# Box sums of the max/average chain by accumulating transfers inside SBUF, and low parts on VectorE, in a fused pooling, convolution and attention kernel

## The reference, cut to what matters

```python
# x: (8, 256, 32, 32)
x_aux = silu(conv1x1(gn(x), w_sta) + b_sta)         # 128 channels
y1 = [x_aux]; y2 = [x_aux]
for _ in range(3):
    y1.append(0.9 * maxpool5x5(y1[-1]) + 0.1 * sumpool5x5(y1[-1]) / 25)    # the max/average chain
    y2.append(rwpool(y2[-1]))                        # exp-weighted pooling, 5x5
y = concat([silu(conv1x1(concat(y1), w_cv1)), silu(conv1x1(concat(y2), w_cv2))])   # 512 channels
a = depthwise 1x3, 3x1, dilated 1x3, dilated 3x1 of y
a = conv1x1(a, w_c1)
x = x + silu(conv1x1(y * a, w_cvend))
f = tokens(gn(x)); q = f @ w1.T
x = x + from_tokens(softmax(q @ f.T / 16) @ (f @ w2.T))
```

## Time and profile before

| | us |
|---|---|
| median of 3 runs | 1584.52 (1584.18 to 1590.7) |
| the profiled execution, its own time | 1581.99 |
| its span | 1580.2 |
| mean granted TensorE clock | 0.909 of full |

### The profile page before, as it was taken

The page is one execution under the profiler, slowest core; times in us unless marked ns, Lnnn a source line. Parts: engine busy times, 40 slices in busy tenths (PEclk is TensorE's granted clock), DMA queues, the critical chain, the costliest instruction groups (busy, mean ns, idle before and its releaser), DMA issues.

```text
span 1580.2 us, 19005 instructions
## 1 busy us (share of the span) xinstructions
PE 1315.6 (83%) x7156; PEld 1095.1 (69%) x7156; DVE 1188.2 (75%) x1167; ACT 715.2 (45%) x773; POOL 336.5 (21%) x138
## 2 busy tenths in 40 slices
PE   3647485677399998999889989998998999999797
PEld 1247475674276887688669858975887688778687
DVE  7659496777868987897699769886988697796443
ACT  0346363455235542653375335534642653465233
POOL 0657585750101020102010210201020102012000
PEclk9768687778599999999999999999999999999999
DMA  7323232221000011001000200020011001000100
GB/s 281 128 94 120 80 108 104 69 118 54 0 27 14 1 52 43 14 1 67 28 14 13 82 9 7 14 81 14 1 40 55 14 1 67 27 1 1 54 1 27
DMA packets 22656, 76.10 MB, mean 48 GB/s; under 512 B 1968, under 2 KB 4656, under 8 KB 22576
## 3 DMA queue, kind: packets, MB, share of 16 engines
q1 hardware_dynamic: 21872, 74.59, 13.0%
q10 hardware_dynamic: 704, 0.30, 0.1%
HBM read 49.71 MB, written 25.17 MB: 47 GB/s over the span
## 4 chain that ended last, share of the span: by engine, by line
issue 55%; PE 11%; POOL 6%; DVE 5%; ACT 1%; POOLq 0%; DVEq 0%; ACTq 0%
POOL q_all L1050 4%; PE slot L1170 3%; PE slot L1132 3%; PE ps_o L1170 2%; POOL f_all L1059 2%; DVE a L1445 2%; DVE between L1445 2%; PE slot L1186 1%; PE slot L1110 0%; POOL c_rstd L1055 0%; PE slot L533 0%; DVE c_minus_max L1454 0%; PE ps_ot L1202 0%; ACT a L1302 0%; ACT pooled L1311 0%
## 5 line engine op out<-in xcount | busy, mean ns | idle before, releaser
L1170 PE MATMUL slot<-f_all,q_all 128*128 128x512 f32 x768 | 193.5, 403 | 13.4 <-ACT pooled L1311 13.4
L1170 PE MATMUL ps_o<-v_all,pt_all 128*128 128x256 f32 x1536 | 200.2, 287 | 5.4 <-ACT mixed L1330 5.2
L1050 POOL TENSOR_TENSOR q_all<-a,f_all 128x1024 fp32r<-128x1024 f32 x32 | 81.4, 2580 | 537.1 <-ACT f_all L1321 537.1
L1445 DVE SCALAR_TENSOR_TENSOR a<-between,k_columns,a 128x992 f32<-128x992 f32 (+1 forms) x128 | 191.5, 1502 | 4.9 <-ACT a L1302 2.6
L1170 PEld LDWEIGHTS ps_o<-v_all,pt_all 128*128 128x128 f32 x1536 | 189.8, 192 | 7.6 <-DVE pt_all L1449 6.2
L1170 PEld LDWEIGHTS slot<-f_all,q_all 128*128 128x128 f32 x768 | 142.7, 192 | 43.1 <-ACT pooled L1311 14.8
L1325 ACT CAST v_all<-y 128x1024 fp32r<-128x1024 f32 x32 | 33.6, 1051 | 191.3 <-DVE y L1467 191.3
L1110 PE MATMUL slot<-wide,k_cv 128*128 128x512 f32 x256 | 114.3, 597 | 0.0
L1449 DVE TENSOR_TENSOR pt_all<-slot,pt_all 128x1024 fp32r<-128x1024 f32 x64 | 78.1, 1221 | 47.6 <-ACT pt_all L1316 47.6
L533 PE MATMUL ps_e<-box,e_hi 128*128 128x192 f32 (+2 forms) x240 | 45.0, 349 | 72.6 <-DVE newton L766 45.2
L1055 POOL TENSOR_TENSOR c_rstd<-c_spread,k_minus_half 128x2 f32<-128x2 f32 x8 | 5.6, 696 | 463.6 <-DVE gmean L1506 463.6
(11 more groups left out here) (163 smaller groups left out, 3019.1 us busy)
## 6 DMA issues: line engine op xcount, KB each, us to landing
y_in<-levels SPq DMA_DIRECT2D x24, 512.0 KB, 3.6
levels<-y_out SPq DMA_DIRECT2D x24, 512.0 KB, 2.7
x_all<-in_x SPq DMA_DIRECT2D x8, 1024.0 KB, 13.2
q_all<-levels SPq DMA_DIRECT2D x8, 1024.0 KB, 4.9
x<-in_x SPq DMA_DIRECT2D x8, 1024.0 KB, 4.9
out<-x SPq DMA_DIRECT2D x8, 1024.0 KB, 5.3
wide<-levels SPq DMA_DIRECT2D x8, 512.0 KB, 3.3
pooled<-levels SPq DMA_DIRECT2D x8, 512.0 KB, 3.3
```

Source lines behind the costliest of these rows:

```text
L1050: nc.gpsimd.tensor_tensor(a_lo[:, k], a[:, k], a_hi[:, k].bitcast(F32), ALU.subtract).then_inc(a_lo_done.sem, 1)
L1170: last = nc.tensor.matmul(out, lhs, rhs, start=(n == 0), stop=(n == len(parts) - 1))
L1445: nc.vector.scalar_tensor_tensor(o, u, keep["taps"][:, s, c, tap:tap + 1], o, ALU.mult, ALU.add).then_inc(taps.sem, 1)
```

## The change

For `phase_c`, the box sum of a level is no longer computed on TensorE. ScalarE copies the level into `row_sums` (`begin_rows`), and GpSimd issues four transfers from SBUF to SBUF that add the level, shifted by +1, -1, +2 and -2 words, to that copy (`add_rows`), each after the one before has landed. ScalarE copies the result to `box_sums` (`begin_columns`), and four more transfers add the row sums, shifted by the same numbers of rows (`add_columns`). That is 24 transfers and 6 copies an image. So that a shift by a word doesn't run into the neighbouring row, the levels have two zero words after each row of 32 (`PITCH` 34, `PADDED` 1092 words). `phase_a` computes each stem a second time in this layout and stores it to a second HBM tensor, `padded`; level 0 of the next image is loaded from it into its own tile, `chain.first`, after the present image's whole chain is done, and into `chain.wide` later, as before. The low parts `f_lo` and `a_lo` move from GpSimd to VectorE. All order in the queues around the chain is rewritten: the maxima of level 0 stand first in VectorE's pass, those of level 1 among the attention tiles, the third mixture last. The diff, cut to its core:

```diff
+PITCH = W + 2
+ROWS = H * PITCH
+PADDED = 2 + ROWS + 2
+SHIFTS = (1, -1, 2, -2)
+    def begin_rows(self, act, i, level):
+        if level:
+            wait(act, self.done, i, MIX * level)
+        else:
+            wait(act, self.first_in, i, 16)
+            wait(act, self.done, i - 1, MIX * LEVELS)
+        self.nc.scalar.copy(self.row_sums[:, 0:ROWS], self.source(level)[:, 2:2 + ROWS]).then_inc(self.rows_begun.sem, 1)
+    def begin_columns(self, act, i, level):
+        wait(act, self.rows_added, i, 4 * 16 * (level + 1))
+        self.nc.scalar.copy(self.box_sums[:, 0:ROWS], self.row_sums[:, 0:ROWS]).then_inc(self.columns_begun.sem, 1)
+    def add_rows(self, pool, i, level):
+        for n, d in enumerate(SHIFTS):
+            if n:
+                wait(pool, self.rows_added, i, 16 * (4 * level + n))
+            else:
+                wait(pool, self.rows_begun, i, level + 1)
+            pool.sem_inc(self.gate, 1)
+            pool.dma_start(self.row_sums[:, 0:ROWS], self.source(level)[:, 2 + d:2 + d + ROWS],
+                           accum_op=ALU.add).then_inc(self.rows_added.sem, 16)
...
# phase_a, ScalarE: silu(n, u)
+                nc.scalar.activation(chain.rows_of(stem_rows[u]), image2d(ps[:, u]), ACT.Silu, bias=keep["b_sta"]).then_inc(rows_done, 1)
                 nc.scalar.activation(stem[u][:, :], ps[:, u], ACT.Silu, bias=keep["b_sta"]).then_inc(stem_done, 1)
...
# phase_c, SyncE
                 if chained:
+                    wait(sp, chain.done, i, MIX * LEVELS)
+                    sp.sem_inc(chain.gate, 1)
+                    if attn:
+                        wait(sp, chain.rows_added, i, 4 * 16 * LEVELS)
+                        sp.sem_inc(chain.gate, 1)
+                    sp.dma_start(chain.first[:, :], padded[i + 1]).then_inc(chain.first_in.sem, 16)
                     wait(sp, cv, i, 2 * CT)
                     load_chain(i + 1)
...
# phase_c, GpSimd
             def step(i, conv, attn, chained):
+                if chained:
+                    chain.add_rows(pool, i + 1, 0)
                 if attn:
                     wait(pool, norm, i - 1, 4)
                     nc.gpsimd.tensor_tensor(rstd[:, :], spread[:, :], keep["minus_half"][:, 0:CT], ALU.pow).then_inc(rstd_done.sem, 1)
-                if attn and conv:
-                    for t in range(CT):
-                        wait(pool, f_hi_done, i - 1, t + 1)
-                        nc.gpsimd.tensor_tensor(f_lo[:, t], a[:, t], f_hi[:, t].bitcast(F32), ALU.subtract).then_inc(f_lo_done.sem, 1)
-                if conv:
-                    for n in range(KT):
-                        inputs_lo(i, n)
+                if chained:
+                    chain.add_columns(pool, i + 1, 0)
+                    for level in range(1, LEVELS):
+                        chain.add_rows(pool, i + 1, level)
+                        chain.add_columns(pool, i + 1, level)
...
# phase_c, ScalarE
+                if chained:
+                    chain.begin_rows(act, i + 1, 0)
...
+                        if chained and k == 1:
+                            chain.begin_columns(act, i + 1, 0)
...
-                        if chained and t == TURN_AT + 1:
-                            level_hi(0)
+                        if chained and t == 2:
+                            chain.begin_rows(act, i + 1, 1)
+                        if chained and t == 6:
+                            chain.begin_columns(act, i + 1, 1)
...
                     gated_hi(0)
                     if chained and attn:
-                        level_hi(1)
-                    gated_hi(1)
+                        chain.begin_rows(act, i + 1, 2)
+                    for m in range(1, KT):
+                        gated_hi(m)
...
+                if chained:
+                    if not attn:
+                        chain.begin_rows(act, i + 1, 2)
+                    chain.begin_columns(act, i + 1, 2)
...
# phase_c, VectorE
+                if chained and attn:
+                    level_maxima(0)
                 if attn:
                     small = Steps(dve, norm, i - 1)
                     wait(dve, group_mean, i - 1, 1)
...
-                        if chained and t == TURN_AT + 1:
-                            level_lo(0)
-                        if chained and 0 < t < TILES - 1:
-                            level_maxima(0, *([0, 1] if t == 1 else [t]))
+                        if chained and t == 2:
+                            level_mixture(0)
+                            level_maxima(1, 0, 1)
+                        if chained and 2 < t < TILES - 1:
+                            level_maxima(1, t - 1)
...
                     turned_lo(TILES - 1)
+                    if conv:
+                        for n in range(KT):
+                            inputs_lo(n)
...
                 if chained and attn:
-                    level_lo(1)
+                    level_maxima(1, 6)
+                    level_mixture(1)
...
                     for m in range(CT):
                         nc.vector.bn_aggr(mv[:, m, :], stats[:, m].rearrange("p h s -> p (h s)")).then_inc(bn.sem, 1)
+                if chained:
+                    level_mixture(2)
```

More of the change, by code:

```diff
@@ L185, in maxima @@
     def maxima(self, dve, i, level, *steps):
-        src, pairs, tall = self.inner(level), self.pairs, self.tall
+        alone = isinstance(i, int) and i == 0
+        first = False if alone else level == 0
+        src, pairs, tall = self.rows_of(self.first) if first else self.inner(level), self.pairs, self.tall
         m4, four = image2d(self.work_b[:, :]), image2d(self.work_a[:, 0:N])
@@ L229, in mixture_of_sums, with mixture_of_boxes @@
         self.mixture(dve, 0, level, self.sum_b[:, :, :])
-    def mixture_of_boxes(self, dve, i, level, slot):
-        wait(dve, self.boxed, i, level + 1)
-        self.mixture(dve, i + 1, level, image2d(slot))
+    def mixture_of_boxes(self, dve, i, level):
+        wait(dve, self.columns_added, i, 4 * 16 * (level + 1))
+        boxes = self.box_sums[:, 0:ROWS].rearrange("p (h w) -> p h w", w=PITCH)[:, :, 0:W]
+        self.mixture(dve, i, level, boxes)
 class Pooled:
@@ L283, in split_lo, with phase_a @@
                                      ALU.subtract).then_inc(self.lo_done.sem, 1)
-def phase_a(nc, x, w, consts, keep, levels, rmc, box, chain, pooled):
+def phase_a(nc, x, w, consts, keep, levels, padded, rmc, box, chain, pooled):
     with ExitStack() as ctx:
@@ L300, in phase_a @@
         stem = (pooled.second, chain.work_b)
+        stem_rows = (chain.row_sums, chain.box_sums)
         raw, at = {}, 0
@@ L331, in phase_a @@
         max_done = sem("a_max_done")
+        rows_set, rows_done = sem("a_rows_set"), sem("a_rows_done")
+        rows_stored = [sem(f"a_rows_stored{u}") for u in range(2)]
         box_ready = sem("a_box_ready")
@@ L365, in _ @@
                     store(pair * 2 + u, u)
+            for u in range(2):
+                sp.wait_ge(rows_stored[u], 16 * (B // 2))
         @block.scalar
@@ L430, in _ @@
             nc.gpsimd.memset(keep["minus_half"][:, :], -0.5).then_inc(rstd_done, 1)
+            for u in range(2):
+                nc.gpsimd.memset(stem_rows[u][:, :], 0.0).then_inc(rows_set, 1)
             chain.set_sum_borders()
@@ L861, with phase_c @@
 BEFORE = KT * STAGES - TILES
-TURN_AT, BOX_AT = 1, TILES - 2
 ORDER = (2, 3, 0, 1)
-def phase_c(nc, x, out, keep, levels, box, chain, pooled):
+def phase_c(nc, x, out, keep, levels, padded, chain, pooled):
     with ExitStack() as ctx:
@@ L1087, in claim @@
                     return slots_of[kind, k]
-                def turn_level(level):
-                    wait(pe, *((chain.done, i + 1, MIX * level) if level else (chain.loaded, i + 1, 16)))
-                    slot = claim("zt", level)
-                    for m in range(N // P):
-                        last = nc.tensor.transpose(slot[:, cols(m)], chain.wide[:, level, cols(m)], keep["ident"][:, :])
-                    last.then_inc(chain.turned.sem, 1)
-                def box_level(level):
-                    wait(pe, chain.hi_done, i, level + 1)
-                    slot = claim("zb", level)
-                    box_sum(nc, pe, box, slot, zt_hi, zt_lo,
-                            (chain.lo_done.sem, chain.lo_done.at(i, level + 1))).then_inc(chain.boxed.sem, 1)
                 def cv1(m, between=None):
@@ L1108, in cv1 @@
                                 wait(pe, chain.done, i, MIX * k)
-                            rows = chain.wide[:, k, h * HALF:(h + 1) * HALF]
-                            last = nc.tensor.matmul(slot[:, h * HALF:(h + 1) * HALF], keep["cv1"][:, k, cols(m)], rows,
+                            rows = chain.inner(k)[:, h * (H // 2):(h + 1) * (H // 2)]
+                            last = nc.tensor.matmul(image2d(slot[:, h * HALF:(h + 1) * HALF]), keep["cv1"][:, k, cols(m)], rows,
                                                     start=(k == 0), stop=(k == KT - 1))
@@ L1612, in _, with program @@
```

(4 more changed lines are left out.)

169 lines of the change are left out of this document (73 added, 96 removed).

## The result

The changed kernel takes 1716.8 us (median of 4 runs, 1714.2 to 1722.7) against 1587.2 (4 runs) for the kernel before: 1.082 times as long, 95% interval 1.078 to 1.086. The profiled execution took 1717.15 us with a span of 1715.3.

A forecast was written before the change was run, and what follows sets the result against it. TensorE was taken to bound the image loop (136.6 of 147.6 us). Span 429.3 + 16D + 6(123.2 + 7D) + 197.4 + 6 = 1371.9 + 58D, 1673.5 at D = 5.2, so 1678 us; 8 in 10: 1605 to 1845.

The forecast's parts named there:

- the loop: Rival 1: 24 serial transfers per image bind, pass 34.4 + 23D above D = 5.55, span 839.1 + 154D; chance 0.3.
- D: Time of one accumulating transfer on GpSimd's queue, semaphore to semaphore: taken as 5.2 us, bounds 3.0 and 6.5.
- M: End of VectorE's third mixture in a pass, forecast at s + 116.8 + 4D.
- The formula of a pass, 123.2 + 7D: One image-loop pass: 116.8 + 4D from s to M plus 6.4 + 3D to next s; 159.6 us at D = 5.2.
- s: End of VectorE's c_shift, where a pass's attention starts; forecast M + 6.4 + 3D, 22.0 us behind M.
- ce: TensorE's second output product in a pass; its end was forecast 113.1 us after s, down from 118.8.
- Rival 4: TensorE's clock drops after two new idle stretches per pass, up to 2.3 us each, adding 28: 1706; chance 0.08.
- 512.5 + 6 for stage one: First pass: M of image 1 at 429.3 + 16D, 512.5; plus 6 (bounds 0 and 12) for computing stems twice.
- 6.1 us behind M [...] instead of 20.1: Pass 7, which has no chain: its s comes 6.1 us behind M instead of 20.1, making the tail 197.4.
- The break-even: Transfer time at which change costs nothing: D = 3.5 against a 147.6 us pass, 3.6 for the whole kernel.
- 5.8 us on the way to ce: Gain from s to end of "ce": 3.9 for TensorE's box sums off the path, the rest from low parts.
- 6.3 of 9.3 (3.9 + 2.4): TensorE's box-sum work per pass, 9.3 us: 3.9 on the path ahead of "ce", last box sum's 2.4 behind it.

The follow-up runs named there:

- hybrid_rstd: Changed kernel with level 2 back on TensorE, c_rstd between second and third row transfer of level 0, ScalarE's level-0 box_sums copy one product earlier: 1551.2 us.
- rstd_early: Changed kernel with c_rstd moved on GpSimd's queue from behind the fourth row-transfer issue of level 0 to between the second and third: 1671.5 us.
- plain: Changed kernel with its transfers as plain copies, the adding left out (box sums wrong in content): 1607.4 us.
- no_boxes: Kernel before with low parts on VectorE and the third stage's box sums left out altogether: 1444.0 us, 0.910 of before.
- hybrid_128: hybrid_rstd with 96 unused bytes behind box_sums, so large tensors start at multiples of 128 bytes: 1537.2 us, 0.973 of before.
- after_128: Changed kernel with 96 unused bytes behind box_sums, so large tensors start at multiples of 128 bytes: 1719.0 us.
- after: The changed kernel itself, against the kernel before: 1716.8 us, 1.082 times as long.
- aligned: Changed kernel with 32 unused bytes behind box_sums, so tensors from pairs on start at multiples of 64 bytes: 1711.6 us, 1.081 of before.

## Why the prediction was right, and where it was off

The forecast was 1678 us, and 1716.8 lies in its range and on its side. It forecast 91 us more than before, and 130 were measured. That the result lies in the range is in part luck: the range reached to 1845 for the case of a dearer transfer, with the loop binding. D came out as forecast and the loop didn't bind; the 39 us came from terms beside D. By the formula it would have taken a D of 5.9.

Of the signs, these held: transfers 5 us apart, c_shift 23.4 us behind M (22 forecast), and no wait of VectorE for column sums in the attention tiles. TensorE was busy for 135.3 us of a pass and not 127, with three idle stretches at the border and not two.

**D.** 5.2 taken, 5.17 measured. The reason given, that the destination is read too, fits the plain copies: they halve the DMA engines' share, and land in 3.0 us instead of 4.7, as the slope of the rows had it (1.7 for 544 KB more). The number came out by two errors that cancel. The 5.1 worked out from the 1 MB rows was the time from issue to landing, which measured 4.5 to 4.7, and the 0.5 us from a landing to the next issue was not added to it. The Trainium skill (pages "DMA: Bandwidth & Descriptors", "Anatomy of one DMA", and "Collectives: The Full Stack", "The bandwidth ceiling: the fold count and why AG ≠ RS ≠ AR") gave an estimate of 4.6 for a transfer; the landing, 4.5 to 4.7, agrees with it.

**The formula of a pass, 123.2 + 7D.** Its shape held: two steps changed by experiment gave 8.2 us (for 6.8 expected) and 20.8 (for 4D = 20.7, though by other parts, as told above). Its constant was 5.7 us too small, 165.3 for 159.6, which is 34 of the 42 us by which span and forecast (1715.3, 1673.5) differ. Over the three parts of the pass that ends at M = 1008.40: s to the end of ce took 114.4 for 113.1, ce to M 26.0 for 24.5, and M to s 23.3 for 22.0. From ce to M one cause shows in rows, and I had left it out: the row transfers of level 2 are on the path, since mixture 3 waits for them and not only for "ce". The first of them meets a 1 MB load that SyncE issues at the same time (SyncE's queue, the chain that ended last, ScalarE):

```profile
956.07 0.41 SPq L1086 DMA_DIRECT2D out<-x  x1
960.27 0.38 SPq L1089 DMA_DIRECT2D x<-in_x  x1
...
960.00 9.07 DMA row_sums<-wide
969.63 5.18 DMA row_sums<-wide
975.37 4.86 DMA row_sums<-wide
...
985.51 1.10 ACT L180 COPY box_sums<-row_sums 128x1088 f32<-128x1088 f32 x1 [1.78 <-DMA row_sums<-wide]
```

One transfer takes 9.07 us instead of 4.7 beside the load, and the copy that starts the column sums waits 1.8 us. Whether moving the load away would give this back wasn't tried.

From M to s the path doesn't touch TensorE. The first issue came 5.7 us behind M (5.0 forecast, the 0.5 us ahead of a transfer again), and c_rstd took 1.03 us where 0.7 was forecast.

From s to ce it is the clock, as far as rows show. Rival 4 had it, outside the sum. Behind the wait of 12.2 us for mixture 3 the granted clock is 0.50 of full (845 to 849), 1.2 of 2.4 GHz, and again behind the 6.7 us wait for the normalised input (872.6 to 876); matmuls there take about twice their time:

```profile
844.76 2.07 PE L1144 MATMUL slot<-wide,k_cv 128*128 128x512 f32 x2 [12.15 <-DVE wide L270]
...
857.15 8.81 PE L1144 MATMUL slot<-wide,k_cv 128*128 128x512 f32 x16
872.65 1.22 PE L1204 MATMUL slot<-f_all,k_w_hi 128*128 128x512 f32 x2 [6.69 <-ACT f_all L1373]
```

Sixteen such matmuls take 7.11 us at full clock (at 1515.17), and two of the fp32r ones 0.73 instead of 1.22 (in hybrid_rstd, at 928.80). The products behind 872.65 lose some 2.3 us by it, an estimate from such pairs of rows, enough for the 1.3 us by which the forecast of this part was too short (its 113.1 is 113.0 by its own terms, which changes nothing). The slow matmuls behind mixture 3 fell where TensorE wasn't last, as the text said of most of them. Later passes take up to 167.4 us, the last of them 117.2 from s to ce; this was not taken apart.

**Pass 0.** M(1) was put at 512.5 + 6 for stage one and came at 515.7. Mixture 1 came at 425.0 where 428 was forecast, and from there to M(1) it took 90.7 us for 90.5. VectorE waits 27.4 and 26.2 us for column sums there, as the 16 transfers in the sum imply.

**The tail.** The way from the last M to the end was put at 197.4 and took 207.8. The step that failed is "6.1 us behind M [...] instead of 20.1": in the last pass of the kernel before, s came only 13.2 us behind M, since VectorE ended the third mixture at 1366.9, when TensorE had 4.6 us of cv2 products left, where a middle pass has 11.7. I had carried the distance of a middle pass to one that I had not looked at: 7 us. The other 3 are TensorE at half clock again, s 9.1 behind M instead of 6.1.

**The rivals.** The loop (34.4 + 23D = 153.3 us at 5.17) did not bind, by rstd_early. Its mechanism, VectorE keeping GpSimd from issuing, shows in no row: the row transfers land in 4.7 us at the least and in the median, and the long ones, one in each pass with 8.5 to 9.2 us, begin within 0.4 us of the issue of a 1 MB load. The break-even was put at D = 3.5 for a pass and 3.6 for the whole; plain has D = 3.5 and takes 1.013 of before, 19 us more, so the break-even lies some 0.3 us below 3.5 (19 by 58).

**The prize.** What the text weighed least well is the gain side: box sums off TensorE's path and low parts on VectorE. It put 5.8 us on the way to ce, 1.9 of them for the low parts. The low parts alone gave 3.4 a pass, and no_boxes shows a further 14.7 for the box sums, while 6.3 of 9.3 (3.9 + 2.4) were called on the path and the rest hidden. In the sum it did not show, since the transfers' path, not TensorE's, set M.

## What to carry to other kernels

A transfer chain in the place of engine work is priced by its latency times the links on the path. Each issue that waits for the one before it blocks everything behind it on that queue: look first at which small step stands behind it (here c_rstd, 8 us of a pass for one line moved). Split a bundled change: here one part gave 2% and the rest took 10%. A total that fits a forecast doesn't show that its parts do: compare them stretch by stretch. Before an engine's saved time is called hidden, leave that work out and run it: the bound tells what a replacement may cost.

## What the runs showed of the hardware

- Addresses in SBUF change TensorE's speed. With large tensors at 32 or 64 bytes behind a multiple of 128, six fp32r matmuls of 512 columns with kept weights take 1.56 to 1.57 us, at multiples of 128 they take 1.52: hybrid_128 against hybrid_rstd, after_128 against after, aligned in between. Which operand matters was not separated. The attention's scores showed nothing of it (396 to 397 ns each in both). In a kernel that TensorE bounds, 96 bytes of filler were worth 0.9%, with a mean granted clock of 0.98 instead of 0.95.
- An accumulating transfer of 544 KB within SBUF costs 5.2 us from issue to issue, a plain one 3.5, and GpSimd's issue row is 0.86 us against 0.54.
- VectorE's instructions were not slowed by the transfers: two tap instructions take 2.54 us beside a transfer (at 856.79) and 2.53 without one (at 871.58), and the maxima keep their 1.23. This agrees with the Trainium skill (page "SBUF — State Buffer", section "Who interferes with whom"), by which DMAs have their own ports.
- A transfer is slower beside another one: 9.07 us from issue to landing, instead of 4.7, when a 1 MB load is issued 0.3 us behind it (960.00 and 960.27), 8.5 to 9.2 in all six such places, and 5.54 when the load comes 1.3 us behind it (632.11 and 633.43).
- Behind TensorE's idle stretches of 12.2 and 6.7 us its granted clock was 0.50 of full, 1.2 of 2.4 GHz.
